# Sixteen feed-forward chunks in sixteen slots, the upper stack in two pieces, and three operations on other engines

## The reference

```python
def _ada_rmsnorm(x, t, gamma_w, beta_w):
    gamma = (t @ gamma_w.T)[:, None, :]
    beta = (t @ beta_w.T)[:, None, :]
    return gamma * _rmsnorm(x) + beta
...
def _attention(x, W_q, W_k, W_v, W_o):
    ...
    attn = jax.nn.softmax(scale * jnp.einsum('bnqd,bnkd->bnqk', q, k), axis=-1)
    o = jnp.einsum('bnqk,bnkd->bnqd', attn, v)
    o = o.transpose(0, 2, 1, 3).reshape(b, l, dm)
    return o @ W_o.T

def _swiglu(x, gate_w, hidden_w, out_w, out_b):
    return jax.nn.silu(x @ gate_w.T) * (x @ hidden_w.T) @ out_w.T + out_b
a_alpha = (t @ attn_alpha_w.T)[:, None, :]
x = x + a_alpha * _attention(_ada_rmsnorm(x, t, attn_gamma_w, attn_beta_w), W_q, W_k, W_v, W_o)
f_alpha = (t @ ffn_alpha_w.T)[:, None, :]
return x + f_alpha * _swiglu(_ada_rmsnorm(x, t, ffn_gamma_w, ffn_beta_w), gate_w, hidden_w, out_w, out_b)
...
# second layer
h = x * (scale[:, None, :] * jax.lax.rsqrt(ms + EPS))
u = h @ up_w.T
val, gate = jnp.split(u, 2, axis=-1)
h = val * jax.nn.gelu(gate, approximate=False)
hq = h + jax.lax.stop_gradient(act_quant(h) - h)
wq = down_w + jax.lax.stop_gradient(weight_quant(down_w) - down_w)
y = hq @ wq.T
return y + x
```

## Time and profile before

| | us |
|---|---|
| median of 3 runs | 1107.0 (1106.47 to 1108.77) |
| profiled execution | 1111.97 |
| its span | 1109.9 |
| PE busy | 1039.5 |
| DVE busy | 771.1 |
| ACT busy | 562.0 |
| POOL busy | 346.8 |

### The profile page before, as it was taken

How to read it: one execution, slowest core, us unless ns; L and a number is a source line. 1 busy time by engine, 2 the same in 40 slices (tenths; PEclk the granted TensorE clock), 3 DMA queues, 4 the chain that set the end, 5 groups by cost and what they waited for, 6 DMA issues and landing times.

```text
span 1109.9 us, 19253 instructions
## 1 busy us (share of the span) xinstructions
PE 1039.5 (94%) x6775; PEld 719.9 (65%) x6775; DVE 771.1 (69%) x1557; ACT 562.0 (51%) x1260; POOL 346.8 (31%) x414
## 2 busy tenths in 40 slices
PE   7779889999999999999899999988989999899997
PEld 6324246755775675677467657754878778788775
DVE  5657776678568757966875786677647787466775
ACT  5246656557566655755575566456552333132221
POOL 2401123324242333324133323211332443243331
PEclk9679989999999999999999999999999999999998
DMA  8363524163316315230641533070310111002111
GB/s 261 129 104 112 114 79 135 39 112 101 111 23 127 116 59 106 90 127 12 102 153 59 61 100 131 15 149 20 97 53 29 59 55 32 29 30 63 58 54 38
DMA packets 89375, 92.71 MB, mean 84 GB/s; under 512 B 11856, under 2 KB 86616, under 8 KB 88256
## 3 DMA queue, kind: packets, MB, share of 16 engines
q1 hardware_dynamic: 87248, 89.59, 30.6%
q10 hardware_dynamic: 2032, 1.90, 0.6%
HBM read 61.68 MB, written 29.78 MB: 82 GB/s over the span
## 4 chain that ended last, share of the span: by engine, by line
PE 75%; DMA 8%; DVE 6%; issue 4%; SPq 4%; POOL 1%; ACT 1%; POOLq 0%; DVEq 0%; ACTq 0%
PE gen L1178 30%; PE core L1178 13%; PE pvb L1308 9%; PE core L1267 8%; PE core L1296 7%; DMA kst<-parts_d 6%; SPq L357 4%; PE gen L1520 2%; DVE negmax L936 2%; PE gen L1252 1%; PE pvb L1512 1%; PE pvb L1316 1%; DMA parts_d<-qk 1%; DMA shift_d<-shift 1%; DVE qs L1128 1%
## 5 line engine op out<-in xcount | busy, mean ns | idle before, releaser
L936 DVE TENSOR_REDUCE negmax<-core 128x1 f32<-128x512 f32 x512 | 339.4, 685 | 181.5 <-PE core L1267 180.4
L719 ACT ACTIVATE p<-core 128x512 f32<-128x512 f32 x512 | 278.8, 599 | 147.2 <-PE core L1296 145.9
L1267 PE MATMUL core<-kst,qst 96*128 96x512 bf16 x512 | 201.0, 395 | 36.4 <-DVE negmax L936 18.3
L1178 PE MATMUL gen<-hs,wgh 128*128 128x256 f32 x1536 | 217.6, 292 | 9.6 <-DVE a L993 9.6
L1178 PEld LDWEIGHTS gen<-hs,wgh 128*128 128x128 f32 x1536 | 193.3, 189 | 47.0 <-DVE a L993 14.7
L1178 PE MATMUL core<-wup,hp 128*128 128x512 f32 x768 | 190.6, 397 | 0.9 <-POOL hp L659 0.9
L610 POOL TENSOR_TENSOR a<-a 128x256 fp32r<-128x256 f32 x128 | 94.7, 740 | 289.1 <-ACT a L737 286.6
L1296 PE MATMUL core<-qst,kst 99*128 99x512 bf16 x512 | 157.6, 384 | 2.4 <-DMA qst<-shift_d 1.1
L1178 PEld LDWEIGHTS core<-wup,hp 128*128 128x128 f32 x768 | 140.0, 189 | 29.2 <-issue 0.9
L1267 PEld LDWEIGHTS core<-kst,qst 96*128 96x128 bf16 x512 | 49.5, 97 | 123.4 <-DVE negmax L936 51.7
L1308 PE MATMUL pvb<-p,vst 128*32 128x512 f32 x1024 | 128.0, 619 | 0.0
(11 more groups left out here) (159 smaller groups left out, 1230.6 us busy)
## 6 DMA issues: line engine op xcount, KB each, us to landing
parts_d<-qk SPq DMA_DIRECT2D x30, 384.0 KB, 2.7
v_d<-v SPq DMA_DIRECT2D x8, 1024.0 KB, 4.0
vst<-v_d SPq DMA_DIRECT2D x16, 512.0 KB, 4.8
qst<-parts_d SPq DMA_DIRECT2D x96, 64.0 KB, 2.3
qst<-parts_d SPq DMA_DIRECT2D x48, 128.0 KB, 4.4
kst<-parts_d SPq DMA_DIRECT2D x48, 128.0 KB, 7.5
kst<-parts_d SPq DMA_DIRECT2D x91, 64.0 KB, 2.3
xr<-in_x_dram SPq DMA_DIRECT2D x8, 512.0 KB, 4.1
```

The costliest lines, as they stand in the source:

```text
L719: act.activation(p32[:, ring(b, m), k * S:(k + 1) * S], stb[k], ACT.Exp, scale=SCALE).then_inc(s["exp_"], 1)
L936: dve.tensor_reduce(negmax[:, n // TT, n % TT:n % TT + 1], smb[n % 2], AX_X, ALU.max, negate=True).then_inc(s["smax"], 1)
L1178: last = pe.matmul(out_, l, r, start=start and i == 0, stop=stop and i == len(passes) - 1, **kw)
L1267: pe.matmul(smb[n % 2], qst[0:KROWS, h, q * P:(q + 1) * P], kst[0:KROWS, h, :], start=True, stop=True).then_inc(s["smax_mm"], 1)
```

## The change

The chunks now have one slot each, 13 to 28; the banks of the chunks and of turn 0 are exchanged, so that chunk 0 avoids the banks of v, and the waits at those places follow. The upper stack is loaded in two pieces with four semaphores for the four groups of heads. The first piece of batch i+1 stands behind shift 3 and before the store of v; it needs the scores of batch i up to slot 20. The second piece stands where the whole was. Batch 0 alone has all its turns, and VectorE's part of them, ahead of the slot's maxima; so far that held for turn 0 only.

Three pieces of work change engine. affine of the first norm goes from VectorE to ScalarE, but for batch 0. The addition of x for the first two row tiles goes from VectorE to GpSimd, with a semaphore x1a of its own. The scaling of the second half of y goes from VectorE to a copy on ScalarE (y_out) and a multiplication in place on GpSimd, ahead of the addition that was there. The load of the next alpha waits for that addition (x2_), no longer for the scaling.

```diff
-    T_GH = [T_OT + 13 + n - (n > 5) for n in range(NCH)]
+    T_GH = [T_OT + 12 + n for n in range(NCH)]
...
         def turn_bank(b, g):
-            return gen[(2 if b == 0 else 1, 2, 1, 0)[g]]
+            return gen[(2 if b == 0 else 0, 2, 1, 0)[g]]
         def gh_bank(b, n):
-            return gen[0] if b == B - 1 else gen[n % 2]
+            return gen[0] if b == B - 1 else gen[(n + 1) % 2]
...
+        STACK = ("stack_first", "stack0_ld", "stack1_ld", "stack2_ld")
         def need(eng, name, per, b, k):
...
-            def stack(b, tile):
+            def stack(b, tile, p0=0, p1=2):
...
-                pieces = ((0, GROUP, "stack_first"), (GROUP, HT, "stack0_ld")) if tile == 0 else ((0, HT, "stack1_ld"),)
+                pieces = ((0, GROUP, STACK[2 * tile]), (GROUP, HT, STACK[2 * tile + 1]))[p0:p1]
...
             def load_xr(b):
-                need_sp("x1_", 2, b, 0)
+                need_sp("x1a", 1, b, 0)
+                need_sp("x1_", 1, b, 0)
...
-                    need_sp("yt", 2, last, 0)
+                    need_sp("x2_", 2, last, 0)
...
+                    if prep:
+                        stack(nxt, 1, 0, 1)
...
-                    stack(nxt, 1)
+                    stack(nxt, 1, 1, 2)
...
+            def first_residual(b):
+
+                need(pool, "xr_load", 16, b, 16)
+                need(pool, "x2_st", 16, b, 0)
+                need(pool, "xt_", 2, b, 1)
+                pool.tensor_tensor(x1[:, 0:2, :], xt[0].rearrange("p (t d) -> p t d", t=2), xr[:, 0:2, :], ALU.add).then_inc(s["x1a"], 1)
+
             def second_residual(b, c):
...
+                if c == 1:
+                    y = h32[:, 1, :].rearrange("p (t d) -> p t d", t=2)
+                    pool.tensor_tensor(y, y, al[:, D:2 * D].unsqueeze(1).broadcast_to([P, 2, D]), ALU.mult).then_inc(s["ym"], 1)
+                    need(pool, "ym", 1, b, 1)
...
             def first_norm(b):
...
+                    for b in at(z, T_OP[0] + 1):
+                        first_residual(b)
...
+
+            def affine(b):
+
+                need(act, "cur_set", 1, b, 1)
+                need(act, "x2_", 2, b - 3, 2)
+                for k in range(KD):
+                    need(act, "xt1", KD, b, k + 1)
+                    act.activation(h32[:, k, :], gen[XT_BANK[k]][:, :], ACT.Identity, bias=cur[:, 0, KD + k:KD + k + 1],
+                                   scale=cur[:, 0, k:k + 1]).then_inc(s["h32_1"], 1)
+
+            def y_out(b):
+                need(act, "y_mm", NCH, b, NCH)
+                need(act, "h32_2", KD, b, KD)
+                act.copy(h32[:, 1, :], gen[Y_BANK][:, :]).then_inc(s["yt"], 1)
             def h_hi(b, i, h):
...
+                    for b in at(z, T_DOWN[2 * KF - 1] + 1):
+                        y_out(b)
+                    for b in at(z, T_H1):
+                        if b > 0:
+                            affine(b)
...
                     for b in at(z, T_SQ2):
-                        need(act, "x1_", 2, b, 2)
+                        need(act, "x1a", 1, b, 1)
+                        need(act, "x1_", 1, b, 1)
...
             def qk_rest(b, j):
...
+                if j < 2:
+                    need(dve, ("x1a", "x1_")[j], 1, b - 2, 1)
...
             def first_residual(b, c):
...
-                    need(dve, "xr_load", 16, b, 16)
-                    need(dve, "x2_st", 16, b, 0)
...
-                need(dve, "xt_", 2, b, c + 1)
-                dve.tensor_tensor(x1[:, 2 * c:2 * c + 2, :], tiles(xt[c]), xr[:, 2 * c:2 * c + 2, :], ALU.add).then_inc(s["x1_"], 1)
+                if c == 1:
+                    need(dve, "xr_load", 16, b, 16)
+                    need(dve, "x2_st", 16, b, 0)
+                    need(dve, "xt_", 2, b, 2)
+                    dve.tensor_tensor(x1[:, 2:4, :], tiles(xt[1]), xr[:, 2:4, :], ALU.add).then_inc(s["x1_"], 1)
             def swiglu(b, n):
...
-                    if i == -1 and z == T_TURN[0]:
-                        shift_parts(0, 0)
+                    for g, t in enumerate(T_TURN):
+                        for b in at(z, t):
+                            if b == 0:
+                                shift_parts(b, g)
...
                         for b in at(z, t):
-                            if (b, g) != (0, 0):
+                            if b > 0:
...
-                    for b in at(z, T_DOWN[2 * KF - 1] + 1):
-                        second_scaling(b, 1)
...
                     for b in at(z, T_H1):
-                        need(dve, "cur_set", 1, b, 1)
-                        need(dve, "x2_", 2, b - 3, 2)
-                        affine(b, 1, 0, 1, 0)
+                        if b == 0:
+                            need(dve, "cur_set", 1, b, 1)
+                            affine(b, 1, 0, 1, 0)
...
             def scores_max(b, n):
-                for first, name in ((0, "stack_first"), (TT * GROUP, "stack0_ld"), (TT * HT, "stack1_ld")):
+                for first, name in ((TT * GROUP * g, STACK[g]) for g in range(NG)):
...
-                    need(pe, "qk_r", 2 * KD, b, 2 * KD)
+                    need(pe, "v_h", TT // 2, b, 1)
...
                 if g == 3:
-                    need(pe, "a_", NCH, b - 1, 3)
+                    need(pe, "a_", NCH, b - 1, 4)
...
+                if b == B - 1:
+                    need(pe, "yt", 2, b, 0)
...
+                    need(pe, "qk_r", 2 * KD, b + 2, 3)
+                if n == 1:
...
                     turned = [(b, g) for g, t in enumerate(T_TURN) for b in at(z, t)]
-                    if (0, 0) in turned:
-                        shift_turn(0, 0)
+                    for b, g in turned:
+                        if b == 0:
+                            shift_turn(b, g)
...
-                        if (b, g) != (0, 0):
+                        if b > 0:
...
```

More of the change, by code:

```diff
@@ L242, in build @@
         xa_load xr_load al_load sq1 ms1 rs1 xn1 xt1 h32_1 hh1 hl1
-        qk_mm qk_h qk_r qk_m qk_l v_mm v_h parts0_st parts1_st v_st stack0_ld stack1_ld v0_ld v1_ld
+        qk_mm qk_h qk_r qk_m qk_l v_mm v_h parts0_st parts1_st v_st stack0_ld stack1_ld stack2_ld v0_ld v1_ld
         smax_mm smax shift_t shift_c shift_st shift_ld
         st_mm exp_ pv_mm o_raw o_tr o_rec o_norm
-        o_t oh ol oproj xt_ x1_ x1b sq2 ms2 rs2 xn2 xt2 h32_2 hh2 hl2
+        o_t oh ol oproj xt_ x1a x1_ x1b ym sq2 ms2 rs2 xn2 xt2 h32_2 hh2 hl2
         gh_mm tanh_ u_ a_ ah a_lo y_mm yt x2_ x2_st
```

## The result

The changed kernel takes 1089.49 us (median of 4 runs, 1087.32 to 1094.27), the kernel before 1107.2 us (4 runs, 1106.47 to 1108.77): a ratio of 0.984, 95% interval 0.981 to 0.988. It gained 17.7 us, where the forecast had a gain of 29.8. The time lies in the range (1068 to 1092) and outside the forecast's own range (up to 1086). The profiled execution took 1094.27, the longest of the four, with a span of 1092.2; against the profiled 1111.97 of before that is also 17.7, so the two traces can be compared term by term.

The account below looks back on a forecast made before the run. TensorE, busy 94% of the span, was taken as the bound, so only holes in its row could be won. Gains less costs summed to 29.8 us, giving a median of 1077.2 us, with a range of 1068 to 1092.

Parts of the forecast that it names:

- one chunk a slot: Steady batches, slot 19: moving the first chunk to slot 13 removes six waits for L993, 5.5 us saved, low end 4.5.
- The boundary's wait: Slot 31, y's scaling off VectorE: heads start 0.5 us earlier at each of six boundaries, 3.0 saved, ends 1.5 and 4.
- The first boundary: Batch 0: scores of slot 5 come 5.3 us earlier, with a new 2 us wait; 7.2 saved, ends 4 and 9.5.
- The second boundary: Batch 1: the stack wait of 4.30 and the slow matmuls behind it go; 7.1 us saved, ends 4.5 and 7.5.
- The sign of being wrong that was named: Changed profile: qst<-shift_d among TensorE's waits with more than 3 us would show the forecast wrong.
- later x2: Shift of slot 2, six batches: x2, alpha and v leave directly before it, 0.4 wait each; costs 2.5 us, worst 9.
- the shift chain takes the place: Rival: slot 2's shift lands 2 us late in each of six batches, costing 12 instead of 2.5; 1086.7 us, chance 12%.
- the second and third rivals: Shift chain at slot 2 (1086.7 us, 12%) and the start giving half, 7 less at both boundaries (1084, 8%).
- The two small ones of batch 0: Piece before batch 1's first shift, lengthening slot 26's shift wait of 0.59, cost 1.2 us; and turned first, cost 1.3.
- Turned first: Batch 0, groups 1 to 3 turned before the slot's maxima: TensorE waits for reductions; cost 1.3 us, ends 0 and 2.5.
- The last pass: Last pass: waits for L993 and their echo go, 4.0 us saved, ends 2 and 6; L930's 1.7 stays.
- The stack's split: Upper stack in 64 KB copies, first piece issued after slot 20: six stack waits go, 5.6 us saved, low end 4.5.

Follow-up runs that it names:

- the shift-first pair: Kernels with the shift of slot 2 first, without and with the last scaling of y back on VectorE: 1072.43 and 1075.56 us.
- the affine on VectorE: First norm's affine back on VectorE in all batches, against the kernel with shift of slot 2 first and both v loads behind the shifts: 1071.00 us.
- the kernel with the shift first: Changed kernel with the shift of slot 2 issued ahead of x2's store, alpha's and v's load: 1072.43 us, ratio 0.968.
- y on VectorE: Changed kernel with the last scaling of y back on VectorE, no copy on ScalarE or multiplication on GpSimd: 1082.01 us, ratio 0.976.
- the kernel with the shift first and whole copies: Shift of slot 2 first, with the upper stack in twelve copies of 128 KB at the old place: 1096.13 us, ratio 0.989.
- the changed kernel with late pieces: Changed kernel with both pieces of the upper stack, still 64 KB copies, at the old place behind slot 28: 1087.49 us, ratio 0.983.

## Why the prediction was right in sign and 12 us off

**Where it was right.** The holes of the earlier trace rows are gone as forecast: one chunk a slot removed all six waits for L993 (5.5 and the hidden part), and no upper-stack wait is left (5.6). In the whole stretch from slot 5 of batch 1 to slot 5 of batch 7 (152.19 to 746.63, now 139.58 to 732.98) only 1.0 us was won; with the 16.7 of the term below it is 17.7, where the other terms of the steady batches were 16.5. The boundary's wait went from 1.25 to 0.65, 0.6 in a batch where 0.5 was forecast, and the shift-first pair shows that part at 3.1 us in the median against 3.0. The first boundary: from the shift of slot 26 to that of slot 10 it was 42.85 us and is 35.80 (47.87 to 83.67 after), 7.05 less, where 7.2 less 1.3 was forecast. Within it the wait at slot 5 was 0.65, not 2. The 7.2 were 5.3 for the earlier scores of slot 5, which came 5.35 sooner counted from the shift of slot 26 (25.45 us before, 20.10 after), and 1.9 that no run shows as a term of its own. What the runs showed in its place: 1.70 of the 7.05 lie behind those scores; the wait of 1.47 for L936 is gone, and it is there again with the affine on VectorE (1.47 for L971, at 69.17); the two groups of sixteen matmuls with v took 3.64 (68.99) and 3.39 us (79.16) before and take 1.92 each now (62.15 and 70.39); and the granted clock is 1.00 from 60 to 84 us, where it was 0.72 from 66 to 84. The shift is issued 12.1 us behind the first copy (50.83 to 62.90), nearly as forecast (12.2, from 52.93 to 65.1), only 2.1 us earlier with the whole stretch; its load is in some 0.3 sooner than forecast, and TensorE asks for it 0.9 later:

```profile
62.90 0.61 SPq L435 DMA_DIRECT2D shift_d<-shift  x1
66.18 0.25 SPq L438 DMA_DIRECT2D qst<-shift_d  x1
...
67.97 0.61 PE L1336 MATMUL core<-qst,kst 99*128 99x512 bf16 x2 [0.65 <-DMA qst<-shift_d]
```

The second boundary: from the scores of slot 29 to the output projection of slot 5 it was 23.79 us (128.40 to 152.19) and is 17.64 (121.94 to 139.58), 6.2 less where 7.1 was forecast, although 1.2 us of slower matmuls, counted below, now lie in it.

The sum with the shift's term left out was 32.3, or 1074.7 us; the kernel with the shift first measured 1072.4. "Boundaries 95 to 96 us apart" came true there (95.9), and not in the changed kernel (97.6 to 99.8). The sign of being wrong that was named, more than 3 us of waits for qst<-shift_d, stands there with 13.3.

**The term that failed** is *later x2*, put at 2.5 with an end of 9. The mechanism was named rightly, that x2's store, alpha and v would leave directly before the shift instead of 3 us ahead of it, and two things in it were mis-sized. First, the shift's store was left at the 2.6 us of the earlier trace rows, with only its start moved. But those 2.6 were what was left of the 7.4 us that the three transfers and the shift took together at that boundary; as x2 moved from 4.80 to 2.00 ahead, the store grew to 5.10. The margin behind the load, which was seen and put at under half a microsecond, could not take that. The six waits are 10.8 us as printed (2.24, 1.70, 1.71, 2.14, 1.45 and 1.54) and 11.7 with their hidden part, against 1.4 before (two waits, 0.57 and 0.46). Secondly, no price was put on the clock in this term: four of the six batches show 0.98 for 1.00 in their window, and each of the four is 1.6 us longer than its wait explains, 6.3. Together 16.7 for 2.5, which is 14.2 more than forecast; 12.1 us were missing in all, the terms that came out better having given back the difference. The rival *the shift chain takes the place* is what happened; it was given 12 us in place of 2.5 and a chance of 12%, and lacked the same 6.3 for the clock. The range was said to reach to 1092, where the second and third rivals meet; 9.5 and 7 on top of 1077.2 make 1093.7.

**The two small ones of batch 0** were under-sized too, again without a price for the clock. The wait for the shift of slot 29 grew from 0.59 to 1.90, with 1.2 of slower matmuls behind it, 2.5 in all for 1.2. *Turned first* brought a wait of 1.4 at slot 10 and one of 0.9 at slot 18 with a clock of 0.89 behind it in the window of 92 to 108 us, some 3.3 for 1.3 by estimate; whether it is a loss on the whole stays open, since undoing it moved the median by 0.5 within a spread of 8.

**What was better than forecast.** The last pass: the two waits for L993, and the slower matmuls behind them, fell away, and of the wait for L930 (1.67), which was to stay, only this is left between 915 and 970 us:

```profile
PE gen L1218 <- DVE h L967: 0.7, 1, 0.7
```

From the second wait for hp to that for L930 it was 136.05 us (840.49 to 976.54) and is 128.82 (829.70 to 958.52): 7.2 for a forecast of 4.0. From slot 5 of batch 7 to there 2.9 were lost (93.86, now 96.72): the waits for hp are 2.0 for two where they were 0.9, one of 0.45 for hs is new, and twelve matmuls behind them took 4.42 us where 24 took 5.72. The 7.2 are also why the chunks alone gave 14.0 for an expected 11: there this stretch is 128.48. And 2.4 us of the difference between the two profiled executions arose before the first shift at 48 us, where the change moves next to nothing: in one the twelve L1223 at 42.14 take 2.73 us, in the other (L1263, 41.81) 1.50, the granted clock being 0.50 there in the one and 0.64 in the other (38 to 50 us). The first shift comes between 45.4 and 50.3 us in the fourteen traces, and it comes at 45.89 with only the chunks moved, so this is luck of a single execution.

**What was right for the wrong reason.** The stack's split was forecast from two things, the earlier landing and the place behind slot 20. The place did nothing that a run shows, and of the rest the larger part, as estimated above, is that the first heads have copies and a semaphore of their own. The place had been given the credit for batch 1's 4.30 us, and copies of 64 KB at the old place end that wait as well. The rate didn't decide: it was about the same (114 and 123 GB/s in the two windows above, with 128 and with 64 KB), and the time to the first usable piece was what TensorE waited for.

The profile of before was also misread in one place: the largest shares beside TensorE's 75% are DMA 8% and VectorE 6%, not the copies and their issues (4%). None of the terms of the sum came from it.

By parts, the chunks alone gave 14.0 and the stack alone 16.9, 30.9 together, and the kernel with the shift first, which has all of the change, 35.2; the changed kernel kept 17.7 of it. The gain did not fail to appear: 17 us of it were handed to one 12 KB store.

## What to carry to other kernels

When a change makes a large transfer's source ready later, look at every small transfer behind it on the same queue: here a store's duration in the trace was no constant but largely what was left of the queue ahead of it (1.38, 3.05 and 5.10 us with nothing, 896 KB and 1408 KB directly ahead), and the better unit was the time from the first large issue to the small landing. Issue the small transfer on the critical chain first, and the large ones whose users have time behind it; here that one reordering was worth as much as the whole change before it (17.1 us and 17.7). And split a load where its user needs only the first half, which can pay even if the bytes move no faster and the issues cost more: halves and copies of 64 KB together were worth 24 us here (1096.1 against 1071.7), at 123 GB/s against 114 and with twenty-four issues for twelve.

## What the runs showed of the hardware

The clock: of six waits at the same place in one execution, those of 2.2, 1.7, 1.7 and 2.1 us were followed by a granted clock of 0.62 to 0.65 over 4.5 us, and those of 1.4 and 1.5 by 1.00. The former are means: behind the first of them it is 0.50 from 239 to 242 us and 0.96 from 242 to 244. At each fall the matmuls behind it lost 1.6 us, nearly as much as the wait itself. The length of the wait alone does not decide: with y on VectorE waits of 1.58 and 2.14 at that place were followed by 1.00. Executions of the changed kernel differ in their mean clock as in their time: 1094.27 us at a mean clock of 0.976, 1090.91 at 0.981, 1088.08 at 0.985, 1087.32 at 0.987. Whether the wait is what makes the runs spread is not shown: the kernel with the shift first spread by 0.8 us, but four others without the wait in the steady batches by 3.7 to 8.2.

The DMA engines: the same rows, in packets of 0.9 and 0.8 KB on the mean (1728 for 1.57 MB, 1925 for 1.59), took twice as much of their time in copies of 128 KB as in copies of 64 KB (84% of 14 us, 41% of 13 us) at about the same rate (114 and 123 GB/s). The views are of the kernel with the shift first and whole copies and of the changed kernel with late pieces. Why, no run here shows: the copies differ in size and also in how many heads one of them spans.
